# Mixer start-up and hand-over to the first MLP: a buffer for each raw weight, another order of the weight halves, and three steps of the first MLP block moved

## The chip, the cores and the metric

The kernel runs on one core of one Trainium2 chip. The metric is the device time of one execution in microseconds; for the kernel before, the median of three runs is 1779.31 us (1777.43 to 1783.02).

## What is computed

Four layers in a row on x of 8 batches x 256 tokens x 512, each added to x after a layer norm:

```python
x = x + _layernorm(_L0_attn_ref(_layernorm(x), ...))   # mamba2 mixer, then an MLP of 1792
x = x + _layernorm(_L0_ffn_ref(_layernorm(x), ...))    # SiLU MLP of 1376 with low-rank parts
x = x + _layernorm(_L1_attn_ref(_layernorm(x), ...))   # attention, 32 heads, 8 K/V heads
x = x + _layernorm(_L1_ffn_ref(_layernorm(x), ...))    # looked-up 4-bit or 8-bit weights, by token norm
```

The change touches the mixer and the first steps of its MLP:

```python
h = rmsnorm(hidden_states, ln1_w)
zxbcdt = h @ w_in.T                       # z, xs, Bs, Cs, dt
xBC = silu(conv(xBC) + conv_b)            # causal, 4 taps
att = (Cc Bc^T) * exp(cs_q - cs_k)        # per chunk of 128, 4 heads
Y = att @ Xdt + carried state + D * xs
h = res + (Y * silu(z)) @ w_out.T
mlp = silu(h2 @ gate_w.T) * (h2 @ up_w.T) @ down_w.T
```

## The kernel before

Products are done in single precision by halves: each operand is split into a high half, rounded to fp32r (ScalarE, a Copy), and a low half, the rest (VectorE or GpSimd, a subtraction), and `product` (lines 124 to 128) issues three matmuls, high by high, low by high, high by low. The program of each engine is written out by hand and runs in order; engines wait for one another by semaphores alone.

**The mixer** (`mixer`, lines 161 to 981) handles one batch of 256 tokens per step. In step b the engines work on batch b (scores, decay, state, values, output), batch f = b+1 (projections, convolution, silu), g = b+2 (transposed input, dt) and e = b+3 (loading and norm). Steps run from -2 to 7; -2 and -1 fill the pipeline. Each engine has its own loop over b, with the pieces in the order in which they are written there.

**The mixer's weights** are 14 slices of 128 x 512 (256 KB each): 0 to 9 for the five projections `project(f, 0..4)` (two slices each), 10 to 13 for the output. Slice n is loaded by SyncE, multiplied in place by the norm's weight on GpSimd (`scale_weight`, n under 10, line 291), copied to its high half on ScalarE (`weight_high`, line 392), and its low half is made on VectorE (`weight_low`, line 572). There are four raw buffers, which lie in the tiles `att` and `y`; the load of slice n waits for the low half of slice n-4. The first use of `att` (`exponents(0, 0)`, line 651) therefore waits for all 14 low halves.

Further names at the start: `normalise` and `normalise_again` (lines 587, 593, VectorE), `norm_roots` (lines 296 to 306, GpSimd), `statistics` (line 578, VectorE), `h_turned` (line 903, TensorE) and `h_high`, `h_low` (lines 429, 599), `dt_product`, `steps_out` (line 435, ScalarE), `dt_turned` (line 919), `softplus` and its parts (lines 439, 441; 605 to 624), which end in `av`, for which `cumulate` (line 849, TensorE) waits; `cumulated` (line 628, VectorE), for which `cs_turned` (line 855) waits; `tapped` (line 399, ScalarE) and `convolve` (line 640, VectorE); `kx_split` (line 695), `exponential` (line 450), `weighted` and `side_of` (lines 663, 670, VectorE), `skip_added`, `side_low`, `att_low`, `y_low` (lines 310, 325, 316, 343, GpSimd).

**The hand-over.** In the last two steps pieces of the first MLP group (`mlps`) are mixed in: `tokens` normalises the first block of 512 tokens, `feed` turns it over on TensorE and makes its halves (`feed_low`, line 1406, VectorE), `fed(0)` lets TensorE wait for all four low parts, `gate` and `up` are a unit's first two products (12 matmuls each), and `piece` makes halves of the MLP's weights (line 1471). After the mixer TensorE, VectorE and the others run over `spots()`, one unit at a time; block 1's tokens are normalised by `normalise(1, half)` (line 1395) and fed at the spots (0,0,1) and (0,0,2).

```python
        pe.wait_ge(consts_in, 16)
        pe.wait_ge(wdt_low, 1)
        for b in range(FIRST_STEP + 1, BATCH):
```

## Time and profile before

| | us |
|---|---|
| median of 3 runs | 1779.31 |
| lowest, highest | 1777.43, 1783.02 |
| the profiled execution's own time | 1781.89 |
| its span, first to last instruction | 1780.1 |
| TensorE busy | 1654.3 (93%) |
| VectorE, ScalarE, GpSimd busy | 1084.2, 803.0, 608.7 |
| mean granted TensorE clock | 0.985 |

PE is TensorE's matmuls, DVE VectorE, ACT ScalarE, POOL GpSimd. Times in rows are from the start of the span. The mixer takes the first 295 us or so, both MLPs the time to about 1150 us, attention and the last layer the rest. A matmul's record is longer than its share of the engine, since matmuls overlap; the spacing of their starts is the rate.

### The profile page before, as it was taken

The page shows a single profiled execution, that of the slowest core. Times are in us where ns is not written, and L with a number is a line of the kernel's source. Part 1 is how long each engine was busy: PE and PEld are TensorE (multiplying, and loading weights), DVE is VectorE, ACT ScalarE, POOL GpSimd, SP SyncE. Part 2 cuts the span into 40 slices and gives each one's busy share as a digit, 9 for nine tenths or more (in the row PEclk, how much of TensorE's full clock was granted, in tenths as well). Part 3 has the DMA queues.
Part 4 walks back from the last instruction along what each step waited for, and adds up shares of the span by engine and source line. Part 5 has one row for each costly group of instructions (what it writes and reads, how often), then busy time and mean ns, then how long its engine had stood idle before and what let it go on. Part 6 is the DMA issues. An engine that isn't in the chain of part 4 may idle for free. (4 is left out here: it accounts for less than half of the span.)

```text
span 1780.1 us, 26343 instructions
## 1 busy us (share of the span) xinstructions
PE 1654.3 (93%) x8965; PEld 1378.8 (77%) x8965; DVE 1084.2 (61%) x2298; ACT 803.0 (45%) x1723; POOL 608.7 (34%) x792
## 2 busy tenths in 40 slices
PE   5999999999999999999999999979988989989884
PEld 4898987888888888777877887867877877778773
DVE  7788886525566554665243324656776776777772
ACT  4676763222332222222122222148777677777760
POOL 5455553211111112341111113474344354344322
PEclk9999999999999999999999999989999999999996
DMA  3000011000111111321011112100000000000000
GB/s 126 30 25 13 5 39 46 24 24 22 30 38 30 35 29 40 110 86 43 19 31 39 28 35 70 55 24 13 1 13 1 13 13 1 13 1 13 13 7 19
DMA packets 32968, 54.27 MB, mean 30 GB/s; under 512 B 3840, under 2 KB 9120, under 8 KB 32832
## 3 DMA queue, kind: packets, MB, share of 16 engines
q1 hardware_dynamic: 32832, 52.55, 9.7%
q8 instruction: 74, 1.21, 0.3%
q14 instruction: 62, 0.51, 0.1%
HBM read 43.10 MB, written 9.44 MB: 30 GB/s over the span
## 5 line engine op out<-in xcount | busy, mean ns | idle before, releaser
L1266 POOL TENSOR_TENSOR m_a_lo<-m_prod,m_a_hi 128x512 fp32r<-128x512 f32 x100 | 134.5, 1345 | 636.4 <-ACT m_a_hi L1348 636.4
L1342 ACT ACTIVATE m_prod<-a_ps 128x512 f32<-128x512 f32 x100 | 59.9, 599 | 543.3 <-PE a_ps L128 543.2
L1501 DVE TENSOR_TENSOR m_prod<-m_prod,a_ps 128x512 f32<-128x512 f32 x100 | 68.8, 688 | 383.8 <-ACT m_prod L1342 383.8
L2050 ACT ACTIVATE t_p<-a_ps,t_nmax 128x128 f32<-128x128 f32 (+1 forms) x512 | 181.7, 426 | 71.3 <-DVE t_nmax L2147 70.6
L2147 DVE TENSOR_REDUCE t_nmax<-a_ps 128x2 f32<-128x512 f32 (+1 forms) x192 | 132.0, 688 | 74.6 <-PE a_ps L2228 40.5
L2153 DVE TENSOR_TENSOR t_pT_lo<-a_ps,t_pT_hi 128x512 fp32r<-128x512 f32 x192 | 131.3, 684 | 39.0 <-ACT t_pT_hi L2043 38.3
L2043 ACT ACTIVATE t_pT_hi<-a_ps 128x512 fp32r<-128x512 f32 x192 | 116.7, 608 | 53.7 <-PE a_ps L2237 53.2
L128 PE MATMUL a_ps<-m_hT_hi,m_w_lo 128*128 128x512 f32 x312 | 124.0, 397 | 0.0
L126 PE MATMUL a_ps<-m_hT_hi,m_w_hi 128*128 128x512 f32 x312 | 123.1, 395 | 0.5 <-DVE f_w_lo L1406 0.5
L127 PE MATMUL a_ps<-m_hT_lo,m_w_hi 128*128 128x512 f32 x312 | 123.3, 395 | 0.0
L2237 PE MATMUL a_ps<-consts,t_p 128*128 128x128 f32 x768 | 115.4, 273 | 0.0
L126 PE MATMUL a_ps<-m_hT_hi,q_w 128*128 128x512 f32 x288 | 113.6, 395 | 1.5 <-DVE m_hT_lo L1406 1.5
L128 PE MATMUL a_ps<-m_hT_hi,q_w 128*128 128x512 f32 x288 | 113.9, 395 | 0.0
L127 PE MATMUL a_ps<-m_hT_lo,q_w 128*128 128x512 f32 x288 | 113.8, 395 | 0.0
L2237 PEld LDWEIGHTS a_ps<-consts,t_p 128*128 128x128 f32 x768 | 92.2, 141 | 9.3
L1348 ACT ACTIVATE m_a_hi<-m_prod 128x512 fp32r<-128x512 f32 x100 | 63.3, 633 | 78.4 <-DVE m_prod L1501 78.4
L1418 DVE TENSOR_TENSOR stream<-a_ps,stream 128x512 f32<-128x512 f32 x128 | 79.5, 683 | 28.2 <-PE a_ps L128 28.2
L126 PE MATMUL a_ps<-f_w_hi,a_w_hi 128*128 128x256 f32 x320 | 93.6, 293 | 2.4 <-DVE a_w_lo L572 2.4
L127 PE MATMUL a_ps<-f_w_lo,a_w_hi 128*128 128x256 f32 x320 | 91.3, 285 | 0.0
L128 PE MATMUL a_ps<-f_w_hi,a_w_lo 128*128 128x256 f32 x320 | 91.2, 285 | 0.0
L2258 PE MATMUL a_ps<-t_pT_hi,t_v 128*128 128x256 f32 x256 | 70.5, 298 | 14.9 <-DVE t_pT_lo L2153 14.3
L126 PE MATMUL a_ps<-m_w_hi,m_a_hi 128*128 128x512 f32 x208 | 83.7, 402 | 0.0
(287 smaller groups left out, 4699.6 us busy)
## 6 DMA issues: line engine op xcount, KB each, us to landing
m_raw<-in_w_mlp SPq DMA_DIRECT2D x75, 256.0 KB, 2.7
a_xt<-in_x SPq DMA_DIRECT2D x8, 512.0 KB, 3.8
t_yl<-in_x SPq DMA_DIRECT2D x16, 256.0 KB, 4.2
x_store<-stream SPq DMA_DIRECT2D x4, 1024.0 KB, 5.2
t_yl<-x_store SPq DMA_DIRECT2D x16, 256.0 KB, 2.7
out<-t_yl SPq DMA_DIRECT2D x16, 256.0 KB, 2.0
m_raw<-in_w_attn SPq DMA_DIRECT2D x10, 256.0 KB, 2.8
a_att<-in_w_mixer SPq DMA_DIRECT2D x8, 256.0 KB, 2.8
```

The lines of the kernel that those rows point to most:

```text
L126: pe.matmul(out, w_hi, x_hi, start=first, stop=False)
L127: pe.matmul(out, w_hi, x_lo, start=False, stop=False)
L128: return pe.matmul(out, w_lo, x_hi, start=False, stop=last)
L1266: pool.tensor_tensor(a_lo[:, n % 2, :], prod[:, :], f(a_hi[:, n % 2, :]), ALU.subtract).then_inc(lo, 1)
L1418: dve.tensor_tensor(tile(i, c), ps[:, ACC + c, :], tile(i, c), ALU.add).then_inc(summed, 1)
L1501: dve.tensor_tensor(prod[:, :], prod[:, :], ps[:, U + TURN_AT["unit", n, 0] % 2, :], ALU.mult).then_inc(prodd, 1)
L2043: act.activation(pT_hi[:, u % 2, :], ps[:, T + u % 2, :], ACT.Copy).then_inc(ph, 1)
L2050: last = act.activation(p[:, u % 2, h * width:(h + 1) * width], ps[:, S + u % 2, h * width:(h + 1) * width], ACT.Exp, bias=nmax[:, u % 3, ...
L2147: dve.tensor_reduce(nmax[:, u % 3, 0:heads], ps[:, S + u % 2, :].rearrange("p (h t) -> p h t", h=heads), AX, ALU.max, negate=True).then_in ...
L2153: dve.tensor_tensor(pT_lo[:, u % 2, :], ps[:, T + u % 2, :], f(pT_hi[:, u % 2, :]), ALU.subtract).then_inc(pl, 1)
L2237: mm = pe.transpose(ps[:, T + u % 2, k * P:(k + 1) * P], p[:, u % 2, k * P:(k + 1) * P], ident)
L2258: pe.matmul(out, v(t), of(pT_hi, t), start=fresh and t == 0, stop=False)
```

## The change

1. Each raw slice has a buffer of its own: slices 0 to 3 over `att_hi` and `att_lo`, 4 to 13 over `side_hi` to `y_lo`, which are first written later. A load now waits only for the load four before it. The wait for all 14 low halves moves from `exponents(0, 0)` on VectorE to `y_high(0, 0)` on ScalarE.
2. GpSimd scales slices 2 and 3 before `norm_roots(1)` and not behind it.
3. ScalarE and VectorE make halves 2 to 5 in step -2, behind `h_high` and `h_low`, 6 and 7 at the head of step -1, 8 and 9 behind the first `tapped` (ScalarE) and the second `convolve` (VectorE), and 10 to 13 at the end of step -1: on ScalarE between `exponential(0, 0)` and `softplus(1)`, on VectorE behind `side_of(0, 0)`.
4. In step 6 VectorE does `feed(0, 1)`, the low halves of the block's second half, ahead of `weighted(7, 0)`, `side_of(7, 0)` and `residual(6, 1)`. In step 7 TensorE does `gate(0, 0, 0)` ahead of `state(7)`.
5. At the spot (0,0,1) VectorE does `normalise(1, 1)` right behind the unit's product and not behind `feed_low(1, 0)`.

The same matmuls, copies and subtractions are issued, as often as before.

```diff
@@ -161,3 +161,3 @@
 def mixer(nc, d, consts, stream, hT, m, ps):
-    NW, RAW = 14, 4
+    NW, SCALED = 14, 10
     w_hi = m.sb("a_w_hi", [P, NW, 512], F32R)
@@ -209,2 +209,4 @@
     y_lo = m.sb("a_y_lo", [P, 2, HEADS, P], F32R)
+    raws = ([m.at(f"a_raw_att{k}", [P, DT, P], F32, m.of["a_att_hi"] + 2048 * k) for k in range(4)]
+            + [m.at(f"a_raw_y{k}", [P, DT, P], F32, m.of["a_side_hi"] + 2048 * k) for k in range(NW - 4)])
     RING, SMALL, CSB, YB, SC, MISC = (0, 2), 1, 3, 4, 5, 6
@@ -242,3 +244,7 @@
 
-        return (att, y)[n % RAW // 2][:, n % 2, :, :]
+        return raws[n][:, :, :]
+
+    def raw_there(eng, n):
+
+        eng.wait_ge(raw_in[n % 4], 16 * (n // 4 + 1))
 
@@ -277,5 +283,5 @@
         for n in range(NW):
-            if n >= RAW:
-                sp.wait_ge(w_low, n - RAW + 1)
-            sp.dma_start(raw(n).rearrange("p a b -> p (a b)"), d["w_mixer"][:, n, :]).then_inc(raw_in[n % RAW], 16)
+            if n >= 4:
+                raw_there(sp, n - 4)
+            sp.dma_start(raw(n).rearrange("p a b -> p (a b)"), d["w_mixer"][:, n, :]).then_inc(raw_in[n % 4], 16)
             if n == 3:
@@ -289,3 +295,3 @@
         def scale_weight(n):
-            pool.wait_ge(raw_in[n % RAW], 16 * (n // RAW + 1))
+            raw_there(pool, n)
             pool.tensor_tensor(raw(n), raw(n), ln1.unsqueeze(2).broadcast_to([P, DT, P]), ALU.mult).then_inc(w_scaled, 1)
@@ -350,6 +356,6 @@
                            ln1.unsqueeze(2).broadcast_to([P, DT, HEADS]), ALU.mult).then_inc(fixed_set, 1)
-        scale_weight(0)
-        scale_weight(1)
+        for n in range(4):
+            scale_weight(n)
         norm_roots(1)
-        for n in range(2, 10):
+        for n in range(4, SCALED):
             scale_weight(n)
@@ -387,6 +393,6 @@
         def weight_high(n):
-            if n < 10:
+            if n < SCALED:
                 act.wait_ge(w_scaled, n + 1)
             else:
-                act.wait_ge(raw_in[n % RAW], 16 * (n // RAW + 1))
+                raw_there(act, n)
             act.activation(w_hi[:, n, :], wide(raw(n)), ACT.Copy).then_inc(w_high, 1)
@@ -480,2 +486,4 @@
             wait(act, out_mm, n - 1)
+            if n == 0:
+                act.wait_ge(w_low, NW)
             act.activation(wide(y_hi[:, c]), wide(y[:, c]), ACT.Copy).then_inc(y_h, 1)
@@ -497,4 +505,4 @@
             if b == -1:
-                weight_high(2)
-                weight_high(3)
+                weight_high(6)
+                weight_high(7)
             if there(f_):
@@ -502,4 +510,4 @@
             if b == -1:
-                weight_high(4)
-                weight_high(5)
+                weight_high(8)
+                weight_high(9)
             if there(b):
@@ -509,5 +517,2 @@
                 tapped(f_, 1)
-            if b == -1:
-                weight_high(6)
-                weight_high(7)
             if there(b):
@@ -525,5 +530,2 @@
                 tapped(f_, 2)
-            if b == -1:
-                weight_high(8)
-                weight_high(9)
             if there(g):
@@ -531,2 +533,5 @@
                 h_high(g, 1)
+            if b == -2:
+                for n in range(2, 6):
+                    weight_high(n)
             if there(b):
@@ -557,7 +562,7 @@
                 kx_high_(f_)
-            if b == -1:
-                for n in range(10, NW):
-                    weight_high(n)
             if there(f_):
                 exponential(f_, 0)
+            if b == -1:
+                for n in range(SCALED, NW):
+                    weight_high(n)
             if b == BATCH - 2:
@@ -647,4 +652,2 @@
             wait(dve, att_l, n - 1)
-            if n == 0:
-                dve.wait_ge(w_low, NW)
             for h in range(HEADS):
@@ -712,4 +715,4 @@
             if b == -1:
-                weight_low(2)
-                weight_low(3)
+                weight_low(6)
+                weight_low(7)
             if there(b) and there(e):
@@ -720,5 +723,2 @@
                 convolve(f_, 0)
-            if b == -1:
-                weight_low(4)
-                weight_low(5)
             if there(f_):
@@ -730,4 +730,4 @@
             if b == -1:
-                weight_low(6)
-                weight_low(7)
+                weight_low(8)
+                weight_low(9)
             if there(b):
@@ -744,5 +744,5 @@
                 convolve(f_, 2)
-            if b == -1:
-                weight_low(8)
-                weight_low(9)
+            if b == -2:
+                for n in range(2, 6):
+                    weight_low(n)
             if there(e):
@@ -769,5 +769,2 @@
                 normalise_again(e)
-            if b == -1:
-                for n in range(10, NW):
-                    weight_low(n)
             if there(f_):
@@ -780,2 +777,4 @@
                 residual(b, 0)
+            if b == BATCH - 2:
+                feed(0, 1)
             if there(g):
@@ -785,6 +784,7 @@
                 side_of(f_, 0)
+            if b == -1:
+                for n in range(SCALED, NW):
+                    weight_low(n)
             if there(b):
                 residual(b, 1)
-            if b == BATCH - 2:
-                feed(0, 1)
 
@@ -937,2 +937,4 @@
                 cs_turned(f_)
+            if b == BATCH - 1:
+                gate(0, 0, 0)
             if there(b):
@@ -941,4 +943,2 @@
                 project(f_, 2)
-            if b == BATCH - 1:
-                gate(0, 0, 0)
             if there(b):
@@ -1025,3 +1025,3 @@
                                                        for j in range(2)}
-FEED_AHEAD = (0, 0, 2)
+FIRST_FEED, FEED_AHEAD = (0, 0, 1), (0, 0, 2)
 
@@ -1513,2 +1513,4 @@
                 unit_product(n)
+            if (g, i, j) == FIRST_FEED:
+                normalise(FEED_SPOTS[g, i, j][0], 1)
             for q in before:
@@ -1523,3 +1525,3 @@
                 block_sums(*last)
-            if FEED_SPOTS.get((g, i, j), (0, 1))[1] == 0:
+            if FEED_SPOTS.get((g, i, j), (0, 1))[1] == 0 and (g, i, j) != FIRST_FEED:
                 normalise(FEED_SPOTS[g, i, j][0], 1)
```

What this does to the order of the engines is shown at three places. First, VectorE from its first instructions to the end of step -2 (line 593 and now 598 is `normalise_again`, 572 and now 577 a low half of a mixer weight, 599 and 604 `h_low`). Before:

```order
L593 TENSOR_SCALAR a_xt<-stream,a_rs 128x512 x2
L703 TENSOR_TENSOR a_wdt_lo<-a_wdt,a_wdt_hi 128x16
L578 BN_STATS a_stats<-a_xt 128x6 x2
L582 BN_AGGR a_mv<-a_stats 128x2 x2
L572 TENSOR_TENSOR a_w_lo<-a_att,a_w_hi 128x512 x2
L599 TENSOR_TENSOR f_w_lo<-a_ps,f_w_hi 128x4x128 x2
L587 TENSOR_SCALAR stream<-a_xt,a_mv,a_rs 128x512 x2
L605 TENSOR_TENSOR a_sp<-a_ps,a_vecs 128x8
```

Now:

```order
L604 TENSOR_TENSOR f_w_lo<-a_ps,f_w_hi 128x4x128 x2
L577 TENSOR_TENSOR a_w_lo<-a_raw_att_91,a_w_hi 128x512
L577 TENSOR_TENSOR a_w_lo<-a_raw_att_92,a_w_hi 128x512
L577 TENSOR_TENSOR a_w_lo<-a_raw_y_93,a_w_hi 128x512
L577 TENSOR_TENSOR a_w_lo<-a_raw_y_94,a_w_hi 128x512
L592 TENSOR_SCALAR stream<-a_xt,a_mv,a_rs 128x512 x2
L610 TENSOR_TENSOR a_sp<-a_ps,a_vecs 128x8
```

Four low halves now stand ahead of `normalise(1)` and of `softplus_in(0)`.

Second, VectorE at the turn from step -1 to step 0 (line 697 copies xk, 670 and now 673 is `side_of(0, 0)`, the BN_STATS row is `statistics(3)`). Before, the last four weights' low halves stand ahead of `kx_split(0)`:

```order
L593 TENSOR_SCALAR a_xt<-stream,a_rs 128x512 x2
L572 TENSOR_TENSOR a_w_lo<-a_y,a_w_hi 128x512 x2
L572 TENSOR_TENSOR a_w_lo<-a_att,a_w_hi 128x512 x2
L695 TENSOR_TENSOR a_kx_lo<-a_ps,a_kx_hi 128x384
L697 COPY a_xk<-a_ps 128x128
```

Now they stand behind `side_of(0, 0)`:

```order
L666 SCALAR_TENSOR_TENSOR a_att<-a_att,a_sp,a_ps 128x128 x4
L673 TENSOR_TENSOR a_side<-a_xk,a_dec 128x512
L577 TENSOR_TENSOR a_w_lo<-a_raw_y_99,a_w_hi 128x512
L577 TENSOR_TENSOR a_w_lo<-a_raw_y_100,a_w_hi 128x512
L577 TENSOR_TENSOR a_w_lo<-a_raw_y_101,a_w_hi 128x512
L577 TENSOR_TENSOR a_w_lo<-a_raw_y_102,a_w_hi 128x512
L583 BN_STATS a_stats<-a_xt 128x6 x2
```

They moved past the whole chain from `kx_split(0)` to `side_of(0, 0)` and stand just ahead of step 0.

Third, VectorE at the end of step 6 (line 1406 is `feed_low` of block 0, 691 and now 694 `residual`, 660 and 663 `weighted(7, 0)`). Before:

```order
L1406 TENSOR_TENSOR f_w_lo<-a_ps,f_w_hi 128x4x128 x2
L691 TENSOR_TENSOR stream<-a_ps,stream 128x512
L660 TENSOR_TENSOR a_dec<-a_att,a_sp 128x4
L663 SCALAR_TENSOR_TENSOR a_att<-a_att,a_sp,a_ps 128x128 x4
L670 TENSOR_TENSOR a_side<-a_xk,a_dec 128x512
L691 TENSOR_TENSOR stream<-a_ps,stream 128x512
L1406 TENSOR_TENSOR f_w_lo<-a_ps,f_w_hi 128x4x128 x2
```

Now:

```order
L1406 TENSOR_TENSOR f_w_lo<-a_ps,f_w_hi 128x4x128 x2
L694 TENSOR_TENSOR stream<-a_ps,stream 128x512
L1406 TENSOR_TENSOR f_w_lo<-a_ps,f_w_hi 128x4x128 x2
L663 TENSOR_TENSOR a_dec<-a_att,a_sp 128x4
L666 SCALAR_TENSOR_TENSOR a_att<-a_att,a_sp,a_ps 128x128 x4
L673 TENSOR_TENSOR a_side<-a_xk,a_dec 128x512
L694 TENSOR_TENSOR stream<-a_ps,stream 128x512
```

The second pair of `feed_low` moved from the end of the step to a place ahead of `weighted(7, 0)`.

## Rows read from the trace of the kernel before

**Rows 1.** Windows of core 0: the start, the mixer, the hand-over, both MLPs

```profile
core 0: us, PE busy (x) PEld busy (x) DVE busy (x) ACT busy (x) POOL busy (x), PEclk, DMA share, GB/s
0.00:64.00 64.00, 38.28 (x246) 33.94 (x247) 45.24 (x106) 31.62 (x55) 29.80 (x45) 0.95 0.31 100
64.00:253.00 189.00, 188.66 (x1350) 170.20 (x1348) 154.36 (x401) 127.56 (x222) 101.07 (x102) 1.00 0.06 18
253.00:303.00 50.00, 45.40 (x226) 37.03 (x227) 38.82 (x65) 25.26 (x43) 25.61 (x20) 0.93 0.20 57
303.00:1150.00 847.00, 837.38 (x3689) 676.09 (x3688) 409.92 (x854) 206.75 (x438) 179.47 (x158) 1.00 0.14 41
```

**Rows 2.** Timeline of PE at the start: start us, us, instruction, idle before and releaser

```profile
20.32 0.58 PE L126 MATMUL a_ps<-f_w_hi,a_w_hi 128*128 128x256 f32 x1
...
43.56 0.55 PE L126 MATMUL a_ps<-f_w_hi,a_w_hi 128*128 128x256 f32 x1 [2.43 <-DVE a_w_lo L572]
...
57.88 0.39 PE L849 MATMUL a_ps<-a_sp,consts 128*128 128x8 f32 x2 [3.55 <-DVE a_sp L624]
...
63.59 0.38 PE L855 MATMUL a_ps<-consts,a_sp 128*4 128x128 f32 x2 [0.52 <-DVE a_sp L628]
```

**Rows 3.** Windows, same columns: project(0, 4), project(1, 0), first stretch of the last step

```profile
43.56:48.82 5.26, 5.26 (x24) 5.26 (x25) 2.76 (x6) 0.00 (x0) 0.99 (x1) 0.50 0.51 168
51.42:54.16 2.74, 2.74 (x25) 2.71 (x23) 2.74 (x7) 2.07 (x3) 0.00 (x0) 1.00 0.00 0
271.13:278.10 6.97, 6.96 (x20) 5.68 (x21) 2.60 (x9) 2.75 (x5) 1.42 (x2) 0.51 0.01 2
```

**Rows 4.** Timeline of DVE at the start

```profile
11.90 0.87 DVE L593 TENSOR_SCALAR a_xt<-stream,a_rs 128x512 f32<-128x512 f32 x2
...
21.20 1.73 DVE L593 TENSOR_SCALAR a_xt<-stream,a_rs 128x512 f32<-128x512 f32 x2
...
24.01 1.29 DVE L572 TENSOR_TENSOR a_w_lo<-a_y,a_w_hi 128x512 fp32r<-128x512 f32 x2
...
41.67 1.75 DVE L572 TENSOR_TENSOR a_w_lo<-a_att,a_w_hi 128x512 fp32r<-128x512 f32 x1
...
53.09 0.55 DVE L695 TENSOR_TENSOR a_kx_lo<-a_ps,a_kx_hi 128x384 fp32r<-128x384 f32 x1
...
58.98 0.68 DVE L670 TENSOR_TENSOR a_side<-a_xk,a_dec 128x512 f32<-128x512 f32 x1
59.58 1.28 DVE L578 BATCH_NORM_STATS2 a_stats<-a_xt 128x6 f32<-128x512 f32 x2
```

**Rows 5.** Timeline of POOL at the start

```profile
20.04 2.22 POOL L291 TENSOR_TENSOR a_att<-a_att,a_vecs 128x512 f32<-128x512 f32 x2
...
41.16 3.39 POOL L336 TENSOR_TENSOR a_cT_lo<-a_cT,a_cT_hi 128x512 fp32r<-128x512 f32 x2
...
59.14 1.68 POOL L310 TENSOR_TENSOR a_att<-a_att,a_skip 128x512 f32<-128x512 f32 x1 [14.60 <-DVE a_att L663]
60.78 1.27 POOL L325 TENSOR_TENSOR a_side_lo<-a_side,a_side_hi 128x512 fp32r<-128x512 f32 x1
```

**Rows 6.** Timeline of ACT at the start

```profile
51.07 1.14 ACT L392 ACTIVATE a_w_hi<-a_att 128x512 fp32r<-128x512 f32 x2
```

**Rows 7.** Timeline of PE at the hand-over

```profile
271.13 1.97 PE L815 MATMUL a_ps<-a_csT,a_vecs 4*128 4x128 f32 x8 [1.98 <-DVE f_w_lo L1406]
...
287.90 0.45 PE L126 MATMUL a_ps<-a_w_hi,a_y_hi 128*128 128x512 f32 x1
...
291.40 0.51 PE L126 MATMUL a_ps<-a_w_hi,a_y_hi 128*128 128x512 f32 x1 [0.49 <-POOL a_y_lo L343]
...
301.88 1.23 PE L1563 MATMUL a_ps<-consts,t_xf 128*128 128x128 f32 x8 [0.96 <-DVE t_xf L1395]
```

**Rows 8.** Timeline of DVE and POOL at the hand-over

```profile
269.80 1.28 DVE L1406 TENSOR_TENSOR f_w_lo<-a_ps,f_w_hi 128x512 fp32r<-128x512 f32 x2
...
277.24 1.11 DVE L663 SCALAR_TENSOR_TENSOR a_att<-a_att,a_sp,a_ps 128x128 f32<-128x128 f32 x4
...
282.11 1.73 POOL L325 TENSOR_TENSOR a_side_lo<-a_side,a_side_hi 128x512 fp32r<-128x512 f32 x1
```

More of the change, by code:

```diff
@@ L215, in mixer @@
     vecs_in, consts_in = sem("vecs_in"), sem("consts_in")
-    raw_in = [sem(f"raw_in{n}") for n in range(RAW)]
+    raw_in = [sem(f"raw_in{n}") for n in range(4)]
     x_in = [sem(f"x_in{n}") for n in range(2)]
```

## The prediction

> **What bounds the kernel now.** I began with the windows by stage [rows 1], to see where TensorE has gaps. From 64 to 253 us it is busy 188.66 of 189.00 us, and in both MLPs 837.38 of 847.00 us; there an earlier start moves everything behind it by the same amount, and nothing else can be won. In the first 64 us it is busy for 38.28 us only, and in the 50 us of the hand-over to the MLP for 45.40. The change lies in these two stretches, so they are worked out one by one, and the time after 303 us is taken as unchanged.
>
> In the start the timeline of TensorE [rows 2] names its waits: until 20.32 us (first projection), 2.43 us for VectorE's low halves of weights 8 and 9, 3.55 us for `av(1)`, then 0.52 us for VectorE's `cumulated(1)`. After 63.59 us there is no gap for 190 us. So what decides about the start is when that row comes. Two windows of equal work [rows 3] show the clock: `project(0, 4)`, 24 matmuls behind the 2.43 us gap and a stretch of tiny products, ran at a granted 0.50 (1.2 GHz) and took 5.26 us; `project(1, 0)`, granted 1.00 (2.4 GHz), took 2.74 us. In the hand-over the timeline [rows 7] shows a gap of 1.98 us for `feed_low`, and from there a stretch of 6.97 us at a granted 0.51 [rows 3].
>
> A second thing to see is a price list. VectorE's `normalise_again` pair takes 0.87 us alone and 1.73 us when GpSimd scales weights beside it; a low half takes 0.65 us alone (1.29 for two) and 1.75 us beside GpSimd's subtraction [rows 4]. GpSimd's op is stretched too: 1.7 us each (3.39 for two) and not the 1.27 of line 325 [rows 5]. Work of the two engines that reads SBUF alone goes one after the other, and this change puts six halves and `normalise_again(0)` beside GpSimd's work.
>
> **The start, step by step** (times of the new kernel are mine, worked out from durations in rows 2 to 6).
> Removed: loads no longer wait for low halves, so GpSimd scales without a pause, at 1.11 us a slice (2.22 for two) [rows 5]. DMA is no limit: the start's windows move 100 GB/s on average [rows 1].
> (a) Scaling slices 2 and 3 now covers 11.7 to 14.1 us. `normalise_again(0)`, 0.87 us from 11.90, falls beside both; one op waits for each. I take its end at 14.3 and not 12.8: +1.6 us for `h_turned(0)`, `statistics(1)` and all behind them. Bounds: 0 (no waiting) and 2.
> (b) `norm_roots(1)` on GpSimd ends later by as much, at 19.7; scaling 4 and 5 ends at 21.8, ScalarE's high half 5 at 22.4, and only then comes `steps_out(0)`: `project(0, 0)` starts at 23.1 and not 20.32.
> (c) On VectorE low halves 4 and 5, each beside a scaling, end at 23.8; `normalise(1)`, `softplus_in(0)` and `normalise_again(1)` beside scaling 7, 8, 9 and the skip product end at 28.8. `av(0)` is there at 30.0 and not at 24.1: +5.9 us, and `project(0, 1)` waits for it.
> (d) From here the new order pays back. `project(0, 2)` starts at 33.8 to 34.2 (31.0 before), `h_low(1)` ends at 40.4, `convolve(0, 2)` at 42.7. Low halves 8 and 9 no longer stand between it and `project(0, 4)`, and that starts at 42.9 and not 43.56.
> (e) Its wait is now about as long as `dt_turned(1)` takes to arrive, without the 2.43 us of nothing. If the clock stays at its higher level it takes 2.74 us and not 5.26: it ends at 45.7, 3.1 us earlier.
> (f) The last four halves leave the way to `kx_split(0)`, which starts at 47.0 and not 53.09: -6.1. But ScalarE's four high halves now stand between `exponential(0, 0)` and `softplus(1)`, 4 x 0.57 = 2.3 us [rows 6], on the way to `av(1)`. `side_of(0, 0)` ends at 56.0 and not at 59.6 to 59.7 [rows 4]: -3.7.
> (g) VectorE's four low halves now follow at once, and with them start three GpSimd ops of 1.7, 1.3 and 1.3 us (59.14, 60.78 and the next) [rows 5]. Three halves each end with one of these ops, a period of 1.7 us, the fourth takes 0.6: 5.7 us. `statistics(3)` starts at 61.6 and not 59.58: +2.0. The path from it to the row at 63.59 us is VectorE's alone (4.0 us), so the mixer's dense part starts 2.0 us later. TensorE idles meanwhile.
> A rule of the Trainium skill bears on (g), "SBUF — State Buffer", section "Who interferes with whom": the pair of ports is an exclusive lock for the full instruction, and the one that loses blocks fully. By it the lone durations would add up (about 1.1 left of the first op, 1.3, 1.3 and four times 0.68), 6.4 us, and the start would cost 2.7 us. The rows say a pair takes 1.7 us and not 1.27 + 0.68, so a little overlap is left; I stay with 5.7.
> Sum of the start: +2.0 us. Best case: no op of the two engines waits for the other. Then (a) falls away, (c) shrinks, and the four halves of (g) take 2.4 us: `statistics(3)` starts at 55.8, -3.8 us. Worst case: the clock, below.
>
> **The hand-over, step by step.**
> (h) The second `feed_low` pair (1.28 us) [rows 8] goes ahead of `weighted(7, 0)`. Its high halves are there by 267.1, so it ends at 268.3, and not at 271.08. `fed(0)` is fulfilled before TensorE ends `output(6, 1)` at 269.0: the gap of 1.98 us goes. `weighted(7, 0)` ends at 269.6 and not at 268.4; `scores(7, 1)`, which waits for it, is not reached before 270.2. Cost nothing.
> (i) Without the gap the clock need not fall. The window at 0.51 [rows 3] holds 6.8 us of half speed, some 3.4 us of lost time.
> (j) `gate(0, 0, 0)`, 12 matmuls in 2.8 us, goes ahead of `state(7)`, which ends at 274.5 (275.8 before). Behind it VectorE's `weighted(7, 1)` starts at 275.9 and not 277.24, so GpSimd's chain from there (`skip_added`, `att_low`, `side_low`, `y_low`) gains only 1.3 us. `side_low(7, 1)` ends at 282.6 to 282.9 (283.8 before), and TensorE, which would be there at 281.5, waits for it over a microsecond. `output(7, 0)` starts at 284.6 and not 287.90: -3.3. `output(7, 1)` needs `y_low(7, 1)`, which comes behind the pieces, the statistics, the product and `gate(7, 1)` on VectorE: 288.65 and not 291.40: -2.75.
> (k) `normalise(1, 1)` ahead of `feed_low(1, 0)` takes the 0.96 us gap before the second transposes of block 1 [rows 7]; the tokens' buffer is free by then. `feed_low(1, 0)` moves back by 1.4 us and ends as the transposes do. -0.95.
> Sum: -3.7 us. Bounds: -1.3 (GpSimd's chain alone sets it) and -6.2 (1.98 + 3.3 + 0.95, if nothing new is waited for).
>
> **Sum.** +2.0 - 3.7 = -1.7 us against the profiled execution's 1781.89 us, 1780.2. Its own time is 2.6 us above the median, so against the median it is 1779.31 - 1.7 = 1777.6 us.
>
> **Rivals.**
> A, my forecast, as above: 1777.6. Chance 0.50. For it: each waiting op has its like in rows 4 and 5.
> B, VectorE and GpSimd hardly disturb one another in the new places (ops fall into one another's pauses): start -3.8, hand-over -3.7, 1779.31 - 7.5 = 1771.8. Against it: side by side placement is certain for (a) and (g). For it: the low half at 24.01 took its 0.65 us when GpSimd had paused. Partial forms reach -5.3. Chance 0.22.
> C, the other side: TensorE's clock in the start. Before, `project(0, 0)` and `(0, 1)` ran without a pause between. Now `project(0, 1)` waits 1.7 us for `av(0)`; if the clock has not risen by then, it runs at 1.2 GHz and takes 2.5 us more (5.26 - 2.74) [rows 3], all on the path by `tapped(0, 1)`. And if the clock still falls before `project(0, 4)`, 2.5 us more. It decides from 1.7 us on, so one such projection is enough to be slower than before: +0.8 with one (1780.1), +3.3 with both (1782.6). Chance 0.20.
> D, the hand-over gains its smallest, 1.3 us, since GpSimd's chain holds all: +0.7, 1780.0. Against it: before, TensorE reached `output(7, 0)` without a recorded wait, so the chain had slack. Chance 0.08.
>
> **How the numbers follow.** A measurement of this kernel can tell 0.3%, 5.3 us, from no change. A, C with one projection and D lie within it; B lies beyond it in most of its forms; beyond +5.3 needs both projections of C and the rule's 0.7 with a small hand-over. Faster 0.22, same 0.70, slower 0.08. The range reaches from B, 1771.8, to both projections of C and 0.9 us more for (a) and (g), 1783.5.
>
> **What would show it.** In the new profile: `h_turned(0)` at 14.5 and not 12.96; low halves with 1.2 to 1.8 us; the row of `cs_turned(1)` (63.59 before) at 65.6, below 61 under B; `project(0, 4)` granted 1.00 and over in 2.7 us; four low halves behind `side_of(0, 0)` in 5.7 us. From there to `output(6, 1)` the distance is the same as before. Then no gap before `decays(7, 1)`, granted clock 1.00 through the last step, a new wait for `side_low(7, 1)` or `y_low`, and no gap before the second transposes. I am wrong if `cs_turned(1)` comes before 63.59, or if the hand-over from there gains under 1.3 or over 6.2 us.

## The result, and the profile of the changed kernel

The changed kernel takes 1782.99 us in the median of 13 runs (1781.43 to 1786.63), the kernel before 1779.15 in the 13 runs beside it (1773.78 to 1783.74): ratio 1.0021, 95% interval 1.0012 to 1.0031. It is slower by 3.8 us, where the forecast was 1.7 us faster. That is inside the 0.3% that I called no change, and inside the range, but on the other side. The profiled executions lie closer than the medians: a span of 1780.8 us against 1780.1.

The windows that answer to [rows 1], and one more for the end of the program:

```profile
core 0: us, PE busy (x) PEld busy (x) DVE busy (x) ACT busy (x) POOL busy (x), PEclk, DMA share, GB/s
0.00:64.00 64.00, 38.90 (x243) 34.43 (x243) 46.98 (x94) 31.20 (x55) 30.34 (x43) 0.89 0.30 100
64.00:253.00 189.00, 185.91 (x1310) 167.88 (x1311) 152.73 (x398) 122.78 (x215) 98.67 (x100) 0.98 0.06 18
253.00:303.00 50.00, 47.82 (x269) 39.43 (x268) 41.98 (x78) 30.16 (x53) 28.09 (x22) 1.00 0.18 52
303.00:1150.00 847.00, 836.31 (x3682) 675.25 (x3683) 409.53 (x854) 206.56 (x438) 179.45 (x158) 1.00 0.14 42
1150.00:1780.00 630.00, 544.76 (x3465) 462.15 (x3463) 437.04 (x878) 411.71 (x967) 272.68 (x469) 0.97 0.03 10
```

Read the clock column first. The hand-over went from a granted 0.93 to 1.00, as meant. The start fell from 0.95 to 0.89, and the mixer's dense part, which had 1.00, has 0.98. The column has a blind spot at the start, though. In the kernel before it reads 1.00 from 20 to 24 us, but the matmuls of `project(0, 0)` start 0.21 us apart until 25.4 us, as in the stretches at 0.50, and the same matmuls in `project(0, 1)` start 0.11 to 0.12 us apart:

```profile
24.96 0.41 PE L126 MATMUL a_ps<-f_w_hi,a_w_hi 128*128 128x256 f32 x1
25.18 0.41 PE L127 MATMUL a_ps<-f_w_lo,a_w_hi 128*128 128x256 f32 x1
...
26.15 0.28 PE L126 MATMUL a_ps<-f_w_hi,a_w_hi 128*128 128x256 f32 x1
26.27 0.28 PE L127 MATMUL a_ps<-f_w_lo,a_w_hi 128*128 128x256 f32 x1
```

In the changed kernel the first products run at that slow rate from 18.3 to 23.2 us. So both kernels begin at half rate, the kernel before for longer, and 0.95 against 0.89 overstates the difference. TensorE's timeline at the start, beside [rows 2]:

```profile
30.19 0.39 PE L849 MATMUL a_ps<-a_sp,consts 128*128 128x8 f32 x2 [2.54 <-DVE a_sp L629]
...
44.79 0.39 PE L126 MATMUL a_ps<-f_w_hi,a_w_hi 128*128 128x256 f32 x1
...
55.73 0.60 PE L849 MATMUL a_ps<-a_sp,consts 128*128 128x8 f32 x2 [2.89 <-DVE a_sp L629]
...
67.09 0.59 PE L855 MATMUL a_ps<-consts,a_sp 128*4 128x128 f32 x2 [3.23 <-DVE a_sp L633]
```

The first row waits for `av(0)`, the third for `av(1)`, the fourth is `cs_turned(1)`: 67.09 us, where it was 63.59 and I had said 65.6. The wait of 2.43 us ahead of `project(0, 4)` (44.79) is gone, and 3.23 us of waiting stand ahead of `cs_turned(1)` in place of 0.52. The four stretches that the column gives at half clock, same columns as the windows above:

```profile
24.68:27.65 2.97, 2.97 (x14) 2.67 (x13) 2.94 (x5) 0.27 (x2) 2.97 (x4) 0.50 0.00 0
31.35:34.77 3.42, 3.42 (x19) 3.42 (x18) 2.44 (x7) 0.94 (x2) 0.00 (x0) 0.50 0.00 0
55.25:62.07 6.82, 6.34 (x28) 6.11 (x29) 6.71 (x12) 2.31 (x5) 5.03 (x3) 0.50 0.01 2
65.49:72.31 6.82, 5.22 (x22) 4.85 (x23) 6.82 (x21) 4.15 (x7) 1.79 (x6) 0.50 0.00 1
```

The first lies on `project(0, 0)` and costs nothing, since TensorE waits 2.54 us for `av(0)` behind it. The second lies on `project(0, 1)`. The third costs nothing either: TensorE waits 3.23 us afterwards. A second execution of the changed kernel (e16) shows it, since there the clock is 1.00 in that place, TensorE waits longer, and `cs_turned(1)` comes no earlier:

```profile
67.07 0.59 PE L855 MATMUL a_ps<-consts,a_sp 128*4 128x128 f32 x2 [6.16 <-DVE a_sp L633]
```

```profile
55.00:63.00 8.00, 5.19 (x37) 4.47 (x37) 7.80 (x13) 4.36 (x7) 5.02 (x3) 1.00 0.01 2
```

The fourth lies behind `cs_turned(1)`, in the part without gaps, and is lost for good. VectorE and GpSimd behind `side_of(0, 0)`, beside [rows 4, 5]:

```profile
56.83 0.69 DVE L673 TENSOR_TENSOR a_side<-a_xk,a_dec 128x512 f32<-128x512 f32 x1
57.43 5.74 DVE L577 TENSOR_TENSOR a_w_lo<-a_raw_y,a_w_hi 128x512 fp32r<-128x512 f32 x4
63.09 1.27 DVE L583 BATCH_NORM_STATS2 a_stats<-a_xt 128x6 f32<-128x512 f32 x2
```

```profile
56.99 1.66 POOL L316 TENSOR_TENSOR a_att<-a_att,a_skip 128x512 f32<-128x512 f32 x1 [9.21 <-DVE a_att L666]
58.61 1.73 POOL L331 TENSOR_TENSOR a_side_lo<-a_side,a_side_hi 128x512 fp32r<-128x512 f32 x1
60.29 1.72 POOL L322 TENSOR_TENSOR a_att_lo<-a_att,a_att_hi 128x512 fp32r<-128x512 f32 x1
```

The four low halves take 5.74 us beside GpSimd's three operations; 5.7 were forecast. TensorE's hand-over, beside [rows 7]:

```profile
274.65 1.15 PE L815 MATMUL a_ps<-a_csT,a_vecs 4*128 4x128 f32 x8
...
286.70 0.50 PE L126 MATMUL a_ps<-a_att_hi,a_kx_hi 128*128 128x512 f32 x1 [0.23 <-POOL a_att_lo L322]
...
288.04 0.30 PE L126 MATMUL a_ps<-a_side_hi,a_st_hi 128*128 128x128 f32 x1 [0.38 <-POOL a_side_lo L331]
...
289.40 0.45 PE L126 MATMUL a_ps<-a_w_hi,a_y_hi 128*128 128x512 f32 x1
...
292.50 0.50 PE L126 MATMUL a_ps<-a_w_hi,a_y_hi 128*128 128x512 f32 x1
...
301.85 1.03 PE L1565 MATMUL a_ps<-consts,t_xf 128*128 128x128 f32 x8
...
303.98 0.50 PE L126 MATMUL a_ps<-f_w_hi,m_w_hi 128*128 128x512 f32 x1 [1.10 <-DVE m_hT_lo L1406]
```

No gap ahead of `decays(7, 1)` (274.65), `output(7, 0)` at 289.40 and `output(7, 1)` at 292.50, two short new waits for GpSimd, none ahead of the second transposes (301.85), but a new one of 1.10 us for the low halves of the tokens behind them.

Landmarks of TensorE in every profiled execution make the rest readable. `cs_turned(1)` opens the dense part; `cs_turned(2)` is one step later; from there to `cs_turned(7)` every kernel takes 151.2 to 151.5 us; "hand-over" is the distance from `cs_turned(7)` to the first product behind the second transposes (302.87 us in the kernel before, 303.98 in the changed one). All in us:

| kernel | av(0) ends | cs_turned(1) | to cs_turned(2) | hand-over | ratio of medians [95%] |
|---|---|---|---|---|---|
| before, three executions | 24.1, 23.9, 24.1 | 63.6, 62.9, 63.9 | 30.6, 30.3, 30.2 | 57.3, 58.5, 55.2 | 1 |
| changed, two executions | 30.1, 30.1 | 67.1, 67.1 | 32.6, 32.2 | 52.9, 52.8 | 1.0021 [1.0012, 1.0031] |
| e1 new start, old hand-over | 30.1 | 67.7 | 32.5 | 57.3 | 1.0041 [1.0028, 1.0054] |
| e2 old start, new hand-over | 24.1 | 60.1 | 30.3 | 54.5 | 0.9989 [0.9978, 1.0001] |
| e3 own buffers, old orders | 27.7 | 65.3 | 30.3 | 55.2 | 1.0028 [1.0015, 1.0041] |
| e5 the same, GpSimd paced | 24.0 | 62.1 | 30.3 | 58.4 | 0.9993 [0.9984, 1.0003] |
| e8 changed, GpSimd held | 26.9 | 66.2 | 32.4 | 52.8 | 1.0009 [1.0000, 1.0018] |
| e6 changed, last halves moved | 29.9 | 61.2 | 30.6 | 52.8 | 0.9975 [0.9965, 0.9985] |
| e4 changed, waits half filled | 29.9 | 66.8 | 32.7 | 52.8 | 1.0014 [1.0006, 1.0023] |
| e13 changed, waits filled | 30.2 | 66.8 | 30.6 | 52.8 | 0.9995 [0.9985, 1.0005] |
| e7 paced start, new hand-over | 24.0 | 57.7 | 30.6 | 52.8 | 0.9946 [0.9934, 0.9959] |
| e9 its start, old hand-over | 23.9 | 57.3 | 30.6 | 55.1 | 0.9964 [0.9951, 0.9977] |
| e10 its gate moved back | 24.0 | 57.9 | 30.6 | 55.6 | 0.9966 [0.9953, 0.9979] |
| e11 its `normalise(1, 1)` moved back | 23.8 | 57.2 | 30.6 | 52.8 | 0.9949 [0.9929, 0.9968] |
| e12 e7 once more | 23.9 | 57.7 | 30.6 | 52.9 | 0.9942 [0.9926, 0.9959] |

### The profile page after: what moved, and what is told of

Read it like the earlier page. It is cut to its first block and busy times, and to the rows that moved or that the text cites. A ratio compares the mean times of both kernels' runs of the same rounds, so it can differ in the third digit from the quotient of the medians.

```text
span 1780.8 us, 26344 instructions
## 1 busy us (share of the span) xinstructions
PE 1653.7 (93%) x8965; PEld 1379.1 (77%) x8965; DVE 1088.3 (61%) x2298; ACT 802.4 (45%) x1723; POOL 609.2 (34%) x792
```

## The experiments

**The two halves of the change apart (e1, e2).** e1 takes from the changed kernel the three edits at the hand-over; e2 makes those three alone.

Their edits at the hand-over, as e2 adds them and e1 takes them out, in VectorE's program, TensorE's, and VectorE's MLP:

```
                 residual(b, 0)
+            if b == BATCH - 2:
+                feed(0, 1)
...
+            if b == BATCH - 1:
+                gate(0, 0, 0)
             if there(b):
                 state(b)
...
+            if (g, i, j) == FIRST_FEED:
+                normalise(FEED_SPOTS[g, i, j][0], 1)
```

> The new start with the hand-over of before. Theory 1 (the whole loss is the start's: 3.5 us on VectorE's and GpSimd's path to cs_turned(1), and about 2 us of half clock behind it): cs_turned(1) near 67.1 us as in the changed kernel, the dense part 5.5 us late against before, total +5 to +6 us (ratio 1.003). Theory 2 (the start costs the 2.0 us that the forecast gave, and the rest of the loss comes from the hand-over): +2 us (ratio 1.001).

> The start of before with the new hand-over. Theory 1: cs_turned(1) at 63.6 us as before, no gap before decays(7,1), clock 1.00 there; -1 us if the clock's fall at the hand-over of before is not in most of its runs, down to -4.4 us if it is (ratio 0.9975 to 0.9995). Theory 2: 0 to +2 us (ratio 1.000 to 1.001).

e1 took 1785.65 us against the 1777.98 of the kernel before beside it (ratio 1.0041), e2 1775.94 (0.9989, with an interval that just reaches 1). The start is what costs, and more than theory 1 had: the loss is the start's alone, and the hand-over gives part of it back. e2 shows something else: its start is the old one in every instruction and still comes to `cs_turned(1)` at 60.1 us, where three executions of the kernel before have 62.9 to 63.9. The old start varies by 3.7 us with the moments at which the clock falls: at half clock are 54.4 to 57.6 us in e2, 43.9 to 48.8 us in the first execution of the kernel before, and three stretches, at 27, 44 and 57 us, in the other two.

**The buffers alone, and the pace (e3, e5).** e3 has the new buffers and loads and every order as before. e5 adds two lines:

```
 def scale_weight(n):
     raw_there(pool, n)
+    if n >= 4:
+        pool.wait_ge(w_low, n - 3)
```

> Raw weights in buffers of their own, every other order as before. Theory 1 (it is the order that costs, and not the earlier loads): GpSimd ends its scalings earlier, TensorE's waits stay, cs_turned(1) at 63 to 64 us, total -1 to +1 us. Rival (GpSimd's scalings without pauses disturb VectorE wherever they fall): cs_turned(1) at 65 us or later, +2 to +4 us.

> The kernel with only the buffers changed, and GpSimd's scaling of slice n (from 4 on) waits again until the low half of slice n-4 is done; the loads stay early. Theory (the loads cost nothing; GpSimd's scalings without pauses stretch VectorE's small operations of softplus(0), which in the unpaced kernel took 0.84 to 1.0 us each and not 0.11 to 0.17): av(0) at 24 to 24.5 us and not 27.7, total as before, -1 to +1 us (ratio 1.000). Rival (the earlier loads or the other addresses of the buffers cost): +3 to +5 us again (ratio 1.002 to 1.003).

e3 took 1783.45 us (ratio 1.0028): my theory fell and the rival held. Its VectorE timeline, with GpSimd's single row behind it:

```profile
23.33 1.01 DVE L620 TENSOR_SCALAR a_sp<-a_sp 128x8 f32<-128x8 f32 x1
24.37 0.20 DVE L622 RECIPROCAL a_sp<-a_sp 128x8 f32<-128x8 f32 x1
24.49 0.84 DVE L623 SCALAR_TENSOR_TENSOR a_sp<-a_sp 128x8 f32<-128x8 f32 x1
25.36 0.97 DVE L625 SCALAR_TENSOR_TENSOR a_sp<-a_sp 128x8 f32<-128x8 f32 x1
26.36 0.97 DVE L628 TENSOR_TENSOR a_sp<-a_sp 128x8 f32<-128x8 f32 x1
27.36 0.17 DVE L630 SCALAR_TENSOR_TENSOR a_sp<-a_sp 128x8 f32<-128x8 f32 x1
```

```profile
19.72 6.59 POOL L297 TENSOR_TENSOR a_raw_y<-a_raw_y,a_vecs 128x512 f32<-128x512 f32 x6
26.27 1.04 POOL L363 TENSOR_TENSOR a_skip<-consts,a_vecs 128x512 f32<-128x512 f32 x1
```

These are the steps of `softplus_out(0)` on 128x8 numbers. In the kernel before the same steps stand at 22.86 to 24.09 us and take 0.12 to 0.20 us each, since GpSimd waits for a raw buffer just then. Here GpSimd scales six slices without a pause, and four of the steps take 0.84 to 1.01 us, each until a scaling is over. `av(0)` comes 3.6 us later. e5 keeps the early loads and gives GpSimd its pauses back, as its timeline shows:

```profile
24.76 2.36 POOL L299 TENSOR_TENSOR a_raw_y<-a_raw_y,a_vecs 128x512 f32<-128x512 f32 x2 [2.58 <-DVE a_w_lo L582]
```

After 2.58 us of waiting for a low half, slices 6 and 7 are scaled from 24.76 us on, behind `av(0)` at 24.01, and the time is 1779.10 us, ratio 0.9993. So loads and addresses cost nothing that these runs can tell; it is the pace of GpSimd. The old buffers' waits had been a protection of VectorE's short chain.

The changed kernel pays at another place. Its `normalise(1)`, `normalise_again(1)` and the first step of the same chain:

```profile
23.96 2.44 DVE L592 TENSOR_SCALAR stream<-a_xt,a_mv,a_rs 128x512 f32<-128x512 f32 x2
...
27.25 1.73 DVE L598 TENSOR_SCALAR a_xt<-stream,a_rs 128x512 f32<-128x512 f32 x2
28.91 0.16 DVE L617 TENSOR_SCALAR a_sp<-a_sp 128x8 f32<-128x8 f32 x1
```

There the chain comes behind GpSimd's scalings, and its steps keep their 0.11 to 0.20 us. The two normalising pairs are stretched, but no more than in the kernel before, where `normalise_again(1)` has 1.73 us too [rows 4] and `normalise(1)` stands at

```profile
17.91 2.44 DVE L587 TENSOR_SCALAR stream<-a_xt,a_mv,a_rs 128x512 f32<-128x512 f32 x2 [1.14 <-POOL a_rs L306]
```

What is new ahead of `av(0)` is (a), which makes `h_turned(0)` 1.5 us later (14.43 and not 12.96), and low halves 2 to 5, which now come before `normalise(1)`. It starts 6.05 us later, and `av(0)` ends 6.05 us later.

**GpSimd held in the changed kernel (e8),** by two lines in `scale_weight`:

```
+    if n == 6:
+        pool.wait_ge(av_done, 2)
```

> The changed kernel, and GpSimd holds the scaling of slice 6 and all behind it until av(0) is there. Theory: normalise(1), normalise_again(1) and softplus(0) no longer stand beside scalings; normalise_again(1) takes 0.9 and not 1.7 us, the second step of softplus_in 0.15 and not 0.8, av(0) at 28.5 and not 30.1; but low halves 6 to 9 come behind convolve and beside the scalings and may take back 1 to 2 us. Total -1.5 to +1 us against the changed kernel (ratio to before 1.001 to 1.003). Rival (GpSimd's company does not count here): av(0) stays at 30.1.

1780.81 us, ratio 1.0009: 2.2 us won by the medians, just beyond the good end of what was expected. `av(0)` ends at 26.9 and not 30.1, earlier than the 28.5 expected; `normalise_again(1)` takes 0.87 us and `normalise(1)` 0.99. But `cs_turned(1)` gains only 0.9 us: the rest of the gain runs into later waits.

**The last four halves (e6).** High halves 10 to 13 behind `silu_z(0, 3)`, low halves ahead of `kx_split(0)`:

```
             silu_z(f_, 3)
+        if b == -1:
+            for n in range(SCALED, NW): weight_high(n)
...
             normalise_again(e)
+        if b == -1:
+            for n in range(SCALED, NW): weight_low(n)
```

> The changed kernel with the last four halves elsewhere: ScalarE takes them behind silu_z(0,3), VectorE ahead of kx_split(0) as before. Theory (behind side_of(0,0) they cost 5.7 us beside GpSimd, here 2.6 us beside nothing, and ScalarE's 2.3 us leave the way to av(1)): kx_split(0) at 51.5, av(1) at about 56.0, statistics(3) at 57.8 and not 63.09, cs_turned(1) at 61.7 and not 67.1, total 4 to 5 us below the changed kernel (1778 to 1779, ratio to before 0.9995 to 1.0005). Rival (TensorE's clock or another chain holds this stretch): under 2 us below the changed kernel (ratio above 1.001).

1775.45 us, ratio 0.9975, 7.5 us below the changed kernel's median, where 4 to 5 were expected. The same four operations, TensorE's row and where it ends up:

```profile
48.31 2.48 DVE L577 TENSOR_TENSOR a_w_lo<-a_raw_y,a_w_hi 128x512 fp32r<-128x512 f32 x4
```

```profile
61.20 0.38 PE L855 MATMUL a_ps<-consts,a_sp 128*4 128x128 f32 x2 [0.50 <-DVE a_sp L633]
```

They take 2.48 us and not 5.74, with no GpSimd operation beside them; `cs_turned(1)` comes 5.9 us earlier, 5.4 were expected. Beyond that, the step behind it takes 30.6 us and not 32.6: with the 3.23 us of waiting gone, the clock no longer falls. Both belong to the place of the last four halves. This is the largest part of the start's loss. e6 moves ScalarE's four high halves too, and no run moves them alone; `cumulate(1)`, which stands behind them, comes only 0.2 us earlier (55.50 and not 55.73), so most of the gain is VectorE's.

**The clock by itself (e4, e13).** Matmuls whose result nothing reads, written to the idle bank of `values`, in three waits of TensorE; nothing else is changed. These are e4's lines; e13 has `filler(26)` for the 12.

```
                 project(f_, 0)
+                if f_ < 2:
+                    filler((8, 11)[f_])
                 cumulate(f_)
...
+                if f_ == 1:
+                    filler(12)
                 cs_turned(f_)
```

> The changed kernel with matmuls of no use (128x128 by 128x512, result in the idle bank of values) in three of TensorE's waits of the start: 8 before cumulate(0), 11 before cumulate(1), 12 before cs_turned(1). Theory (the clock falls because TensorE stands idle there): granted 1.00 from 28 us on, project(0,1) in 2.7 us, cs_turned(1) at 65.6 us, the row of before's distance behind it, total 3.5 us below the changed kernel and about equal to before (ratio 1.000). Rival (the falls have another cause, or the time is not on the path): granted clock 0.50 in the same stretches, total as the changed kernel or up to 1 us more (ratio 1.002 to 1.003).

> The changed kernel with useless matmuls as in the filled one, but 26 and not 12 ahead of cs_turned(1), so that TensorE's whole wait there is covered (the 12 had left 3.37 us idle, and the clock still fell behind it). Theory (the fall behind cs_turned(1) comes of TensorE's idle time ahead of it): granted 1.00 from 36 us on, the distance from cs_turned(1) to cs_turned of the next step 30.3 us and not 32.6, total 2 us below the filled kernel, 1778 to 1779.5 us (ratio to before 1.000 to 1.0008). Rival (the fall has another cause): 0.50 at 65 to 72 us again, 32.6 us, total as the filled kernel (ratio 1.0014).

TensorE's timeline and the window of 65.6 to 72.4 us, for e4 and then for e13:

```profile
66.80 0.59 PE L855 MATMUL a_ps<-consts,a_sp 128*4 128x128 f32 x2 [3.37 <-DVE a_sp L633]
```

```profile
65.60:72.40 6.80, 5.60 (x24) 5.23 (x25) 6.74 (x20) 4.18 (x7) 1.84 (x5) 0.50 0.00 1
```

```profile
66.78 0.38 PE L855 MATMUL a_ps<-consts,a_sp 128*4 128x128 f32 x2 [0.16 <-DVE a_sp L633]
```

```profile
65.60:72.40 6.80, 6.64 (x49) 5.80 (x48) 6.80 (x21) 4.55 (x9) 1.84 (x5) 1.00 0.02 4
```

e4 fell short of its expectation. The fall at 55 us is gone, but 3.37 us stay idle ahead of `cs_turned(1)`, and behind them the clock is at 0.50 as in the changed kernel. In both kernels some 2 us also stay idle ahead of `av(0)` (2.01 and 2.11), and part of `project(0, 1)` still runs at half clock, so these runs do not show what that stretch costs. In e13 only 0.16 us stay idle; `cs_turned(1)` comes at the same time, the clock is at 1.00, and `cs_turned(2)` is 2.1 us earlier. The times are 1780.74 (ratio 1.0014) and 1778.76 us (0.9995). So the idle time ahead of `cs_turned(1)` causes the fall behind it, and the fall costs 2 us (2.1 at `cs_turned(2)`, 2.0 by the medians). Work that nobody reads makes the changed kernel as fast as the one before.

**The starts once more (e14, e15, e16).**

> The kernel before once more, for its start. Theory (the profiled execution that the forecast stood on had a slow start, 2 to 4 us above most): cs_turned(1) at 60 to 62.5 us and not 63.59, and the step after it 30.3 us later. Rival (63.6 is what this start takes, and the other kernels differ by their own edits): 63.3 to 63.9 us.

> The kernel before a third time. Theory: cs_turned(1) at 60 to 62.5 us. Rival: 63.3 to 63.9 us.

> The changed kernel once more. Theory: cs_turned(1) at 66 to 67.7 us, half clock behind it again, the next step's row 32.5 us later. Rival (the fall behind cs_turned(1) was this one execution's): 30.3 us.

The kernel before has `cs_turned(1)` at 62.86 and 63.85 us, the first between the theory's range and the rival's. So the start of its first profile was not 2 to 4 us slower than most, and the theory falls, though e2 shows that 60.1 is possible. The changed kernel has 67.07 and the fall behind it again. It came in all five executions with the four low halves behind `side_of(0, 0)` and TensorE's wait not filled to its end (changed twice, e1, e4, e8), and in none of the others.

**A version with both lessons (e7, e12).** The kernel before with the new hand-over; slices 0 to 7 rotate through the four old buffers, so GpSimd stays paced until `av(0)`; slices 8 to 13 have buffers of their own, and their halves go where an engine had idle time.

```
-        return (att, y)[n % RAW // 2][:, n % 2, :, :]
+        return (att, y)[n % RAW // 2][:, n % 2, :, :] if n < 8 else late[n - 8][:, :, :]
...
                 statistics(e)
+                weight_low(8)
+                weight_low(9)
...
                 silu_z(f_, 3)
+            if b == -1:
+                for n in range(10, NW):
+                    weight_high(n)
```

> The kernel before with the new hand-over, and buffers of their own for the last six slices only (0 to 7 rotate as before, so GpSimd keeps its pauses until av(0)). Low halves 8 and 9 go in VectorE's idle time ahead of h_low(1), high halves 10 to 13 in ScalarE's idle time behind silu_z(0,3), low halves 10 to 13 in VectorE's 4.3 us of idle time ahead of kx_split(0). Theory: av(0) at 24.1, project(0,4) at 41.2 to 41.6, kx_split(0) at 48 to 49 and not 53.09, cs_turned(1) at 57 to 59; start -2 to -5 us, hand-over -2 us, total 1772 to 1774 us (ratio 0.9960 to 0.9978). Rival (the halves meet GpSimd's operations there too, or the clock takes it back): no gain beyond the hand-over's 2 us (ratio 0.999).

> The kernel with the paced start and the new hand-over once more, as the base for the three beside it: 1770 to 1771 us, ratio to before 0.994 to 0.996.

VectorE's timeline in e7, low halves 8 and 9, 10 to 13, and `kx_split(0)`:

```profile
37.05 1.29 DVE L576 TENSOR_TENSOR a_w_lo<-a_raw_att,a_w_hi 128x512 fp32r<-128x512 f32 x2 [0.95 <-ACT a_w_hi L396]
...
44.82 1.28 DVE L576 TENSOR_TENSOR a_w_lo<-a_raw_att,a_w_hi 128x512 fp32r<-128x512 f32 x2
46.02 1.28 DVE L576 TENSOR_TENSOR a_w_lo<-a_raw_side,a_w_hi 128x512 fp32r<-128x512 f32 x2
47.23 0.55 DVE L699 TENSOR_TENSOR a_kx_lo<-a_ps,a_kx_hi 128x384 fp32r<-128x384 f32 x1
```

1770.44 and 1770.22 us: ratios 0.9946 and 0.9942, 8.4 and 9.7 us below the kernel before beside them, where 1772 to 1774 had been expected. All six halves run at 0.6 us each; `kx_split(0)` is at 47.23 us and not 53.09, `cs_turned(1)` at 57.7. It also varies least: 1769.6 to 1771.3 us in twelve runs.

**The hand-over, part by part (e9, e10, e11),** on top of e7: all three edits undone, the gate alone, `normalise(1, 1)` alone.

> The same start with the whole hand-over of before. Theory (the hand-over's gain is the gap of 1.98 us ahead of decays(7,1) and, where it comes, the half clock behind the gap): the gap and a granted 0.50 behind it are back, 2 to 4.5 us more than the base. Rival (the hand-over's part gains under 1 us, the start all): 0 to +1 us.

> The base with gate(0,0,0) back behind state(7) and nothing else changed. The forecast's step (j) gave the move 3.3 us at output(7,0): then this is 2 to 3 us slower than the base. Theory now (at a full clock the move only changes which of two pieces of equal length comes first; ahead of state(7) the gate delays GpSimd's chain, which waits of 0.2 and 0.4 us in the new profile show): no gap before decays(7,1), output(7,1) at the same distance or up to 1 us nearer, total -1 to +0.5 us against the base.

> The base with normalise(1,1) of the first MLP back behind feed_low(1,0). The forecast's step (k) gave the move 0.95 us. Theory now (the second transposes of block 1 come 1.1 us earlier, but the product behind them waits for the same low halves of the tokens): the transposes 1 us later than in the base, the product behind them in the same place, total -0.3 to +0.3 us. Rival (k): +1 us.

e9 undoes the edits of e1 and e2; e10 moves `gate(0, 0, 0)` alone back behind `project(b + 1, 2)`, e11 `normalise(1, 1)` alone. e9 took 1774.25 us, 4.0 above the base, with the 1.98 us gap and half clock behind it. e10 took 1774.30, as much, and there my new theory was wrong. TensorE's row of `state(7)`:

```profile
266.83 0.79 PE L126 MATMUL a_ps<-a_side_hi,a_kx_hi 128*128 128x512 f32 x1 [1.51 <-POOL a_side_lo L329]
```

With `feed_low` early and the gate behind, TensorE reaches `state(7)` before GpSimd's `side_low(7, 0)` is done and waits 1.51 us, and the clock falls there as it did behind the old gap. The first `gate` is what fills that wait: `feed_low` ahead is worth nothing without it (4.0 us with both, 0 with `feed_low` alone; the gate alone was not run). e11 took 1770.26 us, the same as the base: `normalise(1, 1)` ahead gains nothing, since the product behind the transposes waits for `m_hT_lo` (the 1.10 us above).

## Why the prediction was wrong

**The start was the step that failed:** its sum was +2.0 us at `cs_turned(1)`. Measured in the two profiles it is +3.5 there and +5.5 at `cs_turned(2)`. Two terms were at fault: in (g), the idle time of TensorE was given no price, and it cost 2.0 us of half clock; and (d) was 1 to 2 us too short. Item by item:

- (a) and (b) held: `normalise_again(0)` ends at 14.24 us (14.3), and `project(0, 0)` comes late with it.
- (c) held to 0.1 us: `av(0)` ends at 30.13 (30.0). e8 shows that 3.2 us of it hang on GpSimd's company, a part of which the kernel before had too.
- (d) is 1 to 2 us short. `project(0, 1)` ran at a granted 0.50 for its last 16 matmuls, which was rival C's mechanism at rival C's place; `project(0, 4)` starts at 44.79 and not 42.9. The 16 matmuls start 0.21 and not 0.11 us apart, 1.6 us by my estimate; no run has this stretch at full clock with `av(0)` at 30, so how much of it reaches `project(0, 4)` is not shown.
- (e) held in kind: `project(0, 4)` ran at 1.00, and took 3.0 us for 2.74.
- (f) kept its direction: `kx_split(0)` at 48.85 (47.0), `side_of(0, 0)` ends at 57.51 (56.0), late by what (d) had lost.
- (g) held exactly, 5.74 us for 5.7: a pair takes 1.69 us from start to start, where the lone records add up to 0.68 + 1.27 = 1.95. The Trainium skill, "SBUF — State Buffer", "Who interferes with whom", calls the ports that VectorE and GpSimd share an exclusive lock. The trace agrees in kind, and stays 0.7 us below the 6.4 that the lone durations would add up to.
- What was missing behind (g): I wrote "TensorE idles meanwhile" and gave it no price. That idle time let the clock fall in the dense part, 2.0 us more (e13 against e4). I had priced the clock for gaps in the hand-over and for two projections, and not for the gap that my own sum made longer from 0.5 to 3.2 us.

So +2.0 lacks 1.5 us at `cs_turned(1)`, which fits the half clock on `project(0, 1)` without being shown, and 2.0 us of the clock behind (g), which is shown. Rival C had the right kind of loss. Of its two slow projections one came, `project(0, 1)`; the other, `project(0, 4)`, ran at full clock, and the second loss came behind `cs_turned(1)`. That its 1782.6 lies near the median is in part luck, since the two profiles differ by 1.1 us only at 303 us. B, with no disturbance, was furthest off. And (g) itself, though its size was right, was the wrong choice to accept: e6 does the same work ahead of `kx_split(0)` in 2.48 us. Neither the forecast nor a rival asked whether GpSimd's waits for raw buffers were useful. I had called it "scales without a pause" and looked only at the loads' gain.

**The hand-over came out near its forecast, in part by two errors that cancel.** The forecast was -3.7 us from bounds of -1.3 to -6.2. The two profiles give 57.32 to 52.88 us, -4.4; all old hand-overs in the table have 55.1 to 58.5 and the new ones 52.8 to 52.9, but for e2 with 54.5, where a stretch at a granted 0.50 lies at 252 us (the 58.5 and 58.4 of the old ones have such a stretch at 255 us too); medians give 2.0 (e2) and 4.0 (e9). (h) and (i) are seen: no gap, clock 1.00. Of (j), the new waits for GpSimd are there, 0.23 and 0.38 us. Against the 5.5 us by which all before it is late, `output(7, 0)` comes 4.0 us earlier (287.90 + 5.5 - 289.40), 3.3 forecast, and `output(7, 1)` 4.4 (291.40 + 5.5 - 292.50), 2.75 forecast. (k) is wrong: 0 and not -0.95 (e11). So (j) gave 1.65 us more and (k) 0.95 us less, and (j) gives it only together with (h) (e10). D was not needed.

**The base.** I made the sum against one profile and subtracted it from the median. The profiles differ by 1.1 us at 303 us (303.98 - 302.87) and the medians by 3.8. With the other executions of both kernels the difference there is 0.6 to 3.1 us (303.51 - 302.88 and 303.98 - 300.84), and 2.75 to 3.85 us more, taken at `cs_turned(2)`, where the old start runs as it did in e2. How often the kernel before has which start was not counted, so up to 3 us of the 3.8 are not assigned to a row.

## What to carry to other kernels

A wait can protect somebody. Before taking away an engine's wait for a buffer, list what the engine that shares SBUF with it does in that time; a chain of short, dependent VectorE steps can lose most of a GpSimd operation per step (e3, four steps of six), while `convolve`, which reads PSUM, kept its 0.47 us a step beside two scalings at 27.55 to 29.59 us in the kernel before. Put movable VectorE work where GpSimd is idle, not merely behind the critical path (2.48 against 5.74 us for the same four operations). And price every idle stretch that a change opens on TensorE twice: for itself, and for the clock of the dense part behind it. The last is a risk and no certainty: 3.55 us of waiting ahead of `cumulate(1)` left the clock at 1.00 in one execution of the kernel before, and 3.73 us in the same place were followed by half clock in the other two.

## What the runs showed of the hardware

- A VectorE step on 128x8 numbers, 0.12 to 0.20 us alone, takes 0.84 to 1.01 us beside GpSimd scalings of 128x512 that follow one another without a pause. I had expected this of large operations alone. In the changed kernel, where the scalings end before the chain begins, the same steps take 0.11 to 0.20 us.
- At `cs_turned(1)` the granted clock was at 0.50 behind 3.23 to 3.38 us of idle TensorE (changed, e4, e1) and behind 6.16 us (e16, e8), and at 1.00 behind 0.16 (e13) and 0.50 us (e6), with the same instructions behind it. At the hand-over 1.51 us of idle were enough (e10), while 3.55 us ahead of `cumulate(1)` in the kernel before were not. The length of the gap alone does not decide.
- Ahead of the first fall that it shows, the clock column reads 1.00 even while matmuls of 128x256 start 0.21 us apart (kernel before, 20 to 25.4 us), the spacing of the stretches at 0.50; at 1.00 later on they start 0.11 to 0.12 us apart. The spacing tells the rate there.
- 26 useless 128x512 matmuls in a wait made the kernel 4.2 us faster by the medians (1782.99 to 1778.76), of which 2.1 us can be seen behind `cs_turned(1)`.
